# Reordering the first four tiles of a two-layer linear-attention kernel on all engines

## What is computed

```python
def layer(x, emb, mask, ...):            # twice; B=32 blocks of 128 rows, D=512, emb 32x1024
    xn = layernorm(x) * norm_scale + norm_bias
    q, k, v = xn @ Wq + bq, xn @ Wk + bk, xn @ Wv + bv
    k = masked(k); v = v * valid         # masked rows out
    q = softmax(q, within each head)     # 16 heads in layer 0, 8 in layer 1
    k = softmax(k, over the 128 rows)
    y = q @ (k^T @ v)                    # per head
    scale, shift = split(silu(emb) @ W_film + b_film)
    h = silu(layernorm(y) * film_scale... * (1 + scale) + shift)
    return x + h @ W_out + b_out
```

## Time and profile before

| | before |
|---|---|
| median of 3 runs | 858.17 us (856.25 to 859.12) |
| the profiled execution: its time | 857.14 us |
| its span, first to last instruction | 855.1 us |
| TensorE busy | 838.2 us (98%), 6659 matmuls |
| VectorE, ScalarE, GpSimd busy | 679.3, 603.1, 548.9 us |
| granted TensorE clock, mean | 1.00 |
| DMA, mean over the span | 199 GB/s |

### The profile page before, as it was taken

How to read it: one execution, slowest core, us unless ns; L and a number is a source line. 1 busy time by engine, 2 the same in 40 slices (tenths; PEclk the granted TensorE clock), 3 DMA queues, 4 the chain that set the end, 5 groups by cost and what they waited for, 6 DMA issues and landing times.

```text
span 855.1 us, 20095 instructions
## 1 busy us (share of the span) xinstructions
PE 838.2 (98%) x6659; PEld 719.9 (84%) x6659; DVE 679.3 (79%) x1362; ACT 603.1 (71%) x1442; POOL 548.9 (64%) x741
## 2 busy tenths in 40 slices
PE   7999999999999999999999999999999999999998
PEld 7778888888888888888878888888888888888886
DVE  6987778778788788778887887787788787787766
ACT  5376687686676776686876886776776686676665
POOL 3467766766766666766767667667667666765641
PEclk9999999999999999999999999999999999999999
DMA  8876676766667756555587556656566656566441
GB/s 309 286 225 201 201 218 199 228 216 205 195 210 208 233 197 199 179 165 175 169 247 233 185 172 200 201 180 201 179 204 201 202 186 189 178 194 211 142 160 62
DMA packets 139404, 169.81 MB, mean 199 GB/s; under 512 B 12302, under 2 KB 112006, under 8 KB 139302
## 3 DMA queue, kind: packets, MB, share of 16 engines
q1 hardware_dynamic: 138512, 167.56, 62.5%
q10 hardware_dynamic: 790, 0.98, 0.4%
HBM read 95.61 MB, written 72.88 MB: 197 GB/s over the span
## 4 chain that ended last, share of the span: by engine, by line
PE 83%; DMA 6%; DVE 4%; issue 2%; SPq 2%; POOL 1%; ACT 1%; DVEq 0%; POOLq 0%; ACTq 0%
PE PS L1152 72%; PE PS L1248 6%; PE PS L1232 3%; DMA X<-in_x 2%; DMA XT<-x_turned 1%; DMA x_turned<-XS 1%; DMA k_turned<-KT 1%; DMA QT<-qy_turned 1%; POOL XL L667 0%; SPq L400 0%; PE PS L1322 0%; DMA EK<-k_turned 0%; DVE BNX L1515 0%; PE PS L1276 0%; PE PS L1291 0%
## 5 line engine op out<-in xcount | busy, mean ns | idle before, releaser
L680 POOL TENSOR_TENSOR HL<-H,HH 128x512 fp32r<-128x512 f32 x60 | 77.5, 1292 | 185.3 <-ACT HH L916 185.3
L867 ACT ACTIVATE Z<-QT,FC,FA 128x128 f32<-128x128 f32 x240 | 99.0, 483 | 87.7 <-DMA QT<-qy_turned 87.7
L1152 PE MATMUL PS<-XH,WH_k 128*128 128x256 f32 x512 | 149.8, 293 | 0.7 <-DVE KN L1581 0.7
L1152 PE MATMUL PS<-XL,WH_k 128*128 128x256 f32 x512 | 144.8, 283 | 0.0
L1152 PE MATMUL PS<-XH,WL_k 128*128 128x256 f32 x512 | 144.8, 283 | 0.0
L953 ACT ACTIVATE XN<-X,NBX,RSX 128x512 f32<-128x512 f32 x60 | 48.8, 813 | 85.5 <-POOL NBX L629 85.5
L829 ACT ACTIVATE SK<-SK,KN 128x128 f32<-128x128 f32 x256 | 98.9, 387 | 10.7 <-DVE KN L1581 10.4
L1152 PE MATMUL PS<-WH_o,HH 128*128 128x512 f32 x248 | 101.3, 408 | 2.0 <-issue 1.9
L1152 PE MATMUL PS<-WH_v,XH 128*128 128x512 f32 x256 | 100.8, 394 | 0.0
L1152 PE MATMUL PS<-WH_q,XH 128*128 128x512 f32 x256 | 100.7, 393 | 0.0
L1152 PE MATMUL PS<-WL_v,XH 128*128 128x512 f32 x256 | 100.3, 392 | 0.0
(11 more groups left out here) (171 smaller groups left out, 2106.6 us busy)
## 6 DMA issues: line engine op xcount, KB each, us to landing
qy_turned<-QS SPq DMA_DIRECT2D x60, 512.0 KB, 2.9
QT<-qy_turned SPq DMA_DIRECT2D x240, 128.0 KB, 3.1
EK<-k_turned SPq DMA_DIRECT2D x128, 128.0 KB, 2.8
x_turned<-XS SPq DMA_DIRECT2D x30, 512.0 KB, 3.3
XT<-x_turned SPq DMA_DIRECT2D x120, 128.0 KB, 3.5
k_turned<-KT SPq DMA_DIRECT2D x52, 256.0 KB, 3.8
out_x<-X SPq DMA_DIRECT2D x31, 256.0 KB, 3.2
X<-in_x SPq DMA_DIRECT2D x11, 512.0 KB, 5.3
```

Source lines behind the costliest of these rows:

```text
L680: eng.tensor_tensor(hl_of(o), h_of(o), hh_of(o).bitcast(F32), ALU.subtract).then_inc(pool_hl, 1)
L867: z = eng.activation(z_of(o)[:, c * P:c * P + P].rearrange("p (q n) -> p q n", q=Q), src, ACT.Identity, bias=FC[l][:, c, b:b + 1], scale=F ...
L1152: mm = eng.matmul(dst, left[a](c), right[b](c), start=(c == 0 and a + b == 0), stop=(c == C - 1 and a == 1))
```

## The change

The order of the first four tiles is rewritten on SP, POOL, ACT, PE and DVE. The lists after step 4 stay. Two things are new besides order: chunks 2 and 3 of the key weights are cast by VectorE (`split_high` in its block, semaphore `dve_w`), and five low halves, (0, 0), (0, 1), (1, 0), (1, 1) and (2, 1) of (matrix, chunk), go from VectorE to GpSimd. Mask 1 is loaded by SP instead of ACT. ACT's own loads keep their queue, in another order. The fillers on PE are 10, 1 and 14 instead of 10, 14 and 2.

```diff
--- before.py
+++ after.py
@@ -172,7 +172,7 @@
         pe_tq, pe_ty, pe_a = sem("pe_tq"), sem("pe_ty"), sem("pe_a")
         pe_att, pe_y, pe_film = sem("pe_att"), sem("pe_y"), sem("pe_film")
         pe_fold, act_cp = sem("pe_fold"), sem("act_cp")
-        act_cond, act_w = sem("act_cond"), sem("act_w")
+        act_cond, act_w, dve_w = sem("act_cond"), sem("act_w"), sem("dve_w")
         act_ek, act_eq, act_z, act_t = sem("act_ek"), sem("act_eq"), sem("act_z"), sem("act_t")
         act_v, act_hh, act_xf, act_xh = sem("act_v"), sem("act_hh"), sem("act_xf"), sem("act_xh")
         dve_v, dve_q, pool_xl = sem("dve_v"), sem("dve_q"), sem("pool_xl")
@@ -338,11 +338,20 @@
             elif c == 0:
                 eng.wait_ge(ld_w[w - 1], 16)
 
+        def wait_high(eng, w, c):
+
+            if w == 0 and c >= C // 2:
+                eng.wait_ge(dve_w, c - C // 2 + 1)
+            elif w == 0:
+                eng.wait_ge(act_w, c + 1)
+            else:
+                eng.wait_ge(act_w, C * w - C // 2 + c + 1)
+
         def split_low(eng, w, chunks):
 
             for c in chunks:
                 wait_weights(eng, w, c)
-                eng.wait_ge(act_w, C * w + c + 1)
+                wait_high(eng, w, c)
                 eng.tensor_tensor(WL[w % 4][:, c, :], STAGES[w][:, c, :], WH[w % 4][:, c, :].bitcast(F32),
                                   ALU.subtract).then_inc(low_w[w][c], 1)
 
@@ -502,26 +511,26 @@
             load_first(eng, [1])
             load_x(2)
             load_w(1)
-            load_bias(2)
+            load_w(2)
             load_bias(0)
             load_bias(1)
-            load_w(2)
             load_film(0)
+            load_mask(eng, 1)
             load_x(3)
             wait_split(1)
-
             load_x(4)
+            wait_split(0)
+            load_w(3)
+            load_bias(2)
             write_qy(1)
-            load_film(1)
             write_keys(0)
             read_qy(1)
             place_keys(0)
-            wait_split(0)
-            load_w(3)
+            load_film(1)
+            write_qy(2)
             write_x(2)
-            write_qy(2)
+            read_qy(2)
             read_x(2)
-            read_qy(2)
             write_qy(3)
             write_x(3)
             masks_at(2)
@@ -691,28 +700,33 @@
 
             root_x(0)
             root_x(1)
+            split_low(eng, 0, [0])
+            split_low(eng, 0, [1])
             mask_of_keys(0)
+            split_low(eng, 1, [0])
             root_x(2)
             root_x(3)
+            split_low(eng, 1, [1])
             split_low(eng, 2, [0])
+            split_low(eng, 2, [1])
             normalise_keys(0)
+            mask_of_keys(1)
             queries(0)
+            normalise_keys(1)
             root_x(4)
-            mask_of_keys(1)
-            normalise_keys(1)
             root_x(5)
+            queries(1)
             root_x(6)
-            queries(1)
             normalise_keys(2)
             root_x(7)
+            queries(2)
+            add_bo(0)
             root_x(8)
-            add_bo(0)
-            queries(2)
             root_x(9)
             add_bo(1)
+            split_low(eng, 3, [1])
+            x_low(4)
             root_y(0)
-            x_low(4)
-            split_low(eng, 3, [1])
             normalise_keys(3)
             x_low(5)
             root_y(1)
@@ -960,24 +974,21 @@
                     eng.activation(CTH[n], COND[:, n * D:n * D + D], ACT.Tanh, scale=0.5).then_inc(act_cond, 1)
 
             eng.dma_start(VR, vec_rows).then_inc(ld_vec, 16)
+            load_first(eng, [2])
             load_first(eng, [3])
-            load_first(eng, [2])
             load_mask(eng, 0)
-            eng.dma_start(COND, cond).then_inc(ld_cond, 16)
             eng.dma_start(MI, mask0).then_inc(ld_mask, 16)
             eng.dma_start(MF, mask1).then_inc(ld_mask, 16)
+            eng.dma_start(COND, cond).then_inc(ld_cond, 16)
             split_high(0, [0])
             split_high(0, [1])
-            split_high(0, [2])
-            split_high(0, [3])
             x_turned(0)
             x_turned(1)
             split_high(1, [0])
             split_high(1, [1])
-            cond_tanh()
             split_high(1, [2])
             split_high(1, [3])
-            load_mask(eng, 1)
+            cond_tanh()
             split_high(2, [0])
             split_high(2, [1])
             split_high(2, [2])
@@ -987,22 +998,22 @@
             x_turned(3)
             exp_k(1)
             norm_x(4)
-            exp_k(2)
             norm_x(5)
             conditioning_sums(0)
-            exp_q(0)
+            exp_k(2)
             values(0)
+            values(1)
             norm_x(6)
             norm_x(7)
-            heads(0)
-            values(1)
+            exp_q(0)
             split_high(3, [0])
             split_high(3, [1])
+            exp_k(3)
             split_high(3, [2])
+            heads(0)
             values(2)
-            exp_k(3)
+            x_turned(4)
             norm_y(0)
-            x_turned(4)
             norm_x(8)
             heads(1)
             exp_q(1)
@@ -1365,30 +1376,23 @@
                 mm.then_inc(pe_valid, 1)
 
             eng.wait_ge(pool_const, 2)
-            keep_busy(B_Q, 4)
-            keep_busy(B_Q, 6)
+            keep_busy(B_Q, 10)
+            turn_vectors()
+            keep_busy(B_Q, 1)
             turn_x(0)
-            turn_vectors()
             turn_x(1)
-            keep_busy(B_Q, 2)
-            keep_busy(B_Q, 2)
-            keep_busy(B_Q, 2)
-            keep_busy(B_Q, 2)
-            keep_busy(B_Q, 2)
-            keep_busy(B_Q, 2)
-            keep_busy(B_Q, 2)
+            keep_busy(B_Q, 14)
             keys(0)
             keys(1)
-            keep_busy(B_Q, 2)
+            turn_valid()
+            values(0)
             turn_x(2)
-            turn_valid()
+            turn_x(3)
+            count()
             queries(0)
-            values(0)
+            values(1)
             queries(1)
-            turn_x(3)
-            values(1)
             turn_cond()
-            count()
             keys(2)
             conditioning(0)
             queries(2)
@@ -1729,6 +1733,12 @@
                     last = eng.tensor_scalar(FC[l][:, here, :], G[:, here, :], 0.5, None, ALU.mult)
                 last.then_inc(dve_film, 1)
 
+            def split_high(w, chunks):
+
+                for c in chunks:
+                    wait_weights(eng, w, c)
+                    eng.tensor_copy(WH[w][:, c, :], STAGES[w][:, c, :]).then_inc(dve_w, 1)
+
             def start():
 
                 eng.wait_ge(pool_const, 4)
@@ -1777,62 +1787,59 @@
                 eng.wait_ge(pe_vec, 1)
                 eng.tensor_copy(VC[:, :], PS[:, B_TY, 0:2 * VROWS]).then_inc(dve_vec, 1)
 
+            start()
             stat_x(0)
             stat_x(1)
             norm_x(0)
-            split_low(eng, 0, [0])
+            start_vectors()
             norm_x(1)
-            split_low(eng, 0, [1])
+            split_high(0, [2])
+            split_high(0, [3])
             split_low(eng, 0, [2])
-            start_vectors()
+            x_low(0)
             split_low(eng, 0, [3])
+            x_low(1)
             stat_x(2)
             stat_x(3)
-            x_low(0)
-            x_low(1)
-            split_low(eng, 1, [0])
+            split_low(eng, 1, [2])
+            norm_x(2)
+            split_low(eng, 1, [3])
             start_masks()
-            norm_x(2)
             norm_x(3)
-            split_low(eng, 1, [2])
             keys(0)
-            split_low(eng, 2, [1])
+            start_valid()
             split_low(eng, 2, [2])
-            split_low(eng, 1, [3])
             split_low(eng, 2, [3])
-            split_low(eng, 1, [1])
+            values(0)
             keys(1)
             key_sums(0)
-            queries(0)
-            stat_x(4)
-            values(0)
-            turn_queries(0)
-            stat_x(5)
-            stat_x(6)
-            start()
-            start_cond()
             x_low(2)
             x_low(3)
-            start_valid()
+            queries(0)
             turn_keys(0)
             key_sums(1)
+            start_cond()
+            turn_queries(0)
+            turn_keys(1)
+            values(1)
             start_cond_turned()
+            stat_x(4)
             queries(1)
-            turn_keys(1)
+            stat_x(5)
             zero_attention()
             keys(2)
-            values(1)
             start_count()
             turn_queries(1)
             turn_x(4)
+            turn_x(5)
             key_sums(2)
-            turn_x(5)
+            stat_x(6)
+            queries(2)
             stat_x(7)
+            keys(3)
+            values(2)
             stat_x(8)
             stat_x(9)
-            queries(2)
-            values(2)
-            keys(3)
             mixed(0)
             turn_queries(2)
             conditioning(0)
```

## The result

The changed kernel takes 868.35 us (median of 4 runs, 865.84 to 869.63) against 858.02 (4 runs, 856.25 to 859.12) before: a ratio of 1.0112, 95% interval 1.0092 to 1.0133. It is slower, and by more than the forecast's upper end of 863.6. The profiled execution took 865.84 us, its span is 864.1, TensorE is busy for 839.7 us of it.

A forecast was written before the change was run, and what follows sets the result against it. TensorE, 98% busy, was taken as the bound, so the start of keys(4) shifts everything: 67.6 instead of 64.97, with handovers plus 2.7 us, giving 859.8 profiled and 860.9 median. Range 857.0 to 863.6.

The forecast's parts named there:

- The sign: Whole kernel: the change makes it slower, by plus 2.7 us.
- The film load costs the write of x its lead: SyncE's queue: 2 MB ahead of write_x(2); turned x arrives at 56.0, 1.9 us earlier than before, not 3.8.
- serial line: Turned x to keys(4): x_turned(4), x_low(4), root_y(0), norm_y(0) now run one after another; keys(4) at 67.6 instead of 64.97.
- the part on mix(0): Start of mix(0): heads(0) done at 51.0, mix(0) 0.9 us earlier, TensorE waiting 3.7 us for 0.77.
- minus 5.6, with idle time the same within 0.7, so 46.5: VectorE before mix(0): less work ahead of keys(3) makes it end at 46.5 instead of 52.36.
- 0.9 in keys(0): VectorE: allowance of 0.9 us, in keys(0) alone, for time lost beside GpSimd's low halves.
- five low halves fewer (... 3.25): VectorE before keys(3): five low halves moved to GpSimd save VectorE 3.25 us.
- rival 3: Start of mix(0): heads(0) done by 48, turned x back by 50, lead stays, about 854.4; chance 0.07.
- VectorE has no idle time between 18 and 47: VectorE: the argument against the faster rival, no idle time to win keys(3) 3 us sooner from.
- Neither moves keys(4): VectorE slowed beside GpSimd's low halves, 0.85 or up to 1.3 us each: keys(4) said not to move.
- I find no wait on this way: TensorE up to attention(0): 33.6 us from 13.7 without a wait, attention(0) done at 47.3, 3.8 us ahead.
- Rival 2: keys(4) and neighbours, 62.9 to 67.6: TensorE's clock falls after idle times, 2 to 3 us more, 863.5; chance 0.12.

The follow-up runs named there:

- film_early: Changed kernel with load_film(1) issued by SyncE right behind load_bias(2) instead of behind place_keys(0); ratio 1.0082 against before.
- before_film: Kernel before with load_film(1) issued behind place_keys(0), ahead of the output weights and the write of turned x; ratio 1.0061 against before.
- before_y: Kernel before with x_turned(4) ahead of norm_y(0) on ScalarE and x_low(4) ahead of root_y(0) on GpSimd; ratio 1.0086 against before.
- second trace: Kernels before and after each run once more unchanged, one run each; keys(4) at 65.11 in before and 69.85 in after.
- low_back: Changed kernel with the five low halves back on VectorE, the rest of the change kept; ratio 1.0096 against before.
- heads_early: Changed kernel with heads(0) on ScalarE right behind exp_q(0), ahead of the output chunks and exp_k(3); ratio 1.0124 against before.
- y_first: Changed kernel with norm_y(0) ahead of x_turned(4) on ScalarE and root_y(0) ahead of x_low(4) on GpSimd; ratio 1.0064 against before.
- y_first_fillers: y_first with twenty fillers between attention(0) and mix(0); ratio 1.0025 against before.
- before_wo: Kernel before with the output weights loaded right behind x4 instead of behind place_keys(0); ratio 0.9987 against before.
- best: all_three with root_y(0) also ahead of add_bo(1) on GpSimd and six fillers before mix(0); ratio 1.0022 against before.
- all_three: Changed kernel with the edits of film_early, y_first and heads_early together; ratio 1.0047 against before.

## Why the prediction was wrong

**What held.** The sign, and the mechanism. keys(0) came at 12.4 with its second pair of chunks at 13.7 (forecast 13 and 13.7), keys(1) ended near 19 (19.5). The film load costs the write of x its lead (film_early and before_film; 1.7 to 4.2 us at turned x, by the traces compared). The orders of x and y make a serial line of 11.9 us for 11.6, and undone they give back 3.65 at keys(4); before_y shows 3.95 for them alone. keys(4) waits for x_low(5), and output(0) shifts with film(0).

**The step that failed** is VectorE's sum in the part on mix(0): "minus 5.6, with idle time the same within 0.7, so 46.5". It was 49.56, 3.1 us later. (The terms give 46.7; 0.2 of it is arithmetic.) The idle time was about right. After x_low(1), up to the end of keys(3), VectorE waits 2.06 us in before and 2.38 in after. What the sum lacked is that instructions grow long beside GpSimd's. It had this once, as 0.9 in keys(0), which before has too. Three more places cost 3.0 us in after: norm_x(3) 1.51 for 0.55 beside the low half (1, 1); start_cond's two 1.08 and 1.52 for 0.67 each beside queries(0) and normalise_keys(1); the last of keys(3) 0.96 for 0.16 beside queries(2). The second trace has the same (1.50, 1.08 and 1.52, 0.96). The first two, 2.2 us, lie ahead of turn_queries(0), which ends at 34.13 for 31.8, and of stat_x(7), 2.4 late. That GpSimd is the cause is shown for norm_x(3), and for KB, which low_back brings back to 0.53 and 0.16; for the others it is argued from what ran beside them. VectorE's timeline of before, for comparison:

```profile
33.41 0.67 DVE L1756 SCALAR_TENSOR_TENSOR XS<-Z,XS 32x512 f32<-32x512 f32 x1
34.01 0.67 DVE L1756 SCALAR_TENSOR_TENSOR XS<-EQ,XS 32x512 f32<-32x512 f32 x1
...
49.96 0.69 DVE L1620 TENSOR_TENSOR VV<-PS,BB 128x512 f32<-128x512 f32 x1 [0.80 <-PE PS L1152]
```

Nor did the term "five low halves fewer (... 3.25)" buy anything in the new order: low_back has them back and ends at the same time, because without them VectorE waits for other engines. And rival 3's "VectorE has no idle time between 18 and 47" is not what before shows: its waits there come to 1.1 us.

From there it went three ways:

- *To the queue.* turn_queries(0) was late, so write_qy(1) went out at 34.16 for 31.8, and behind it load_film(1) at 41.35 for 38.6. write_qy(2) and write_x(2) wait for transposes of their own on the same late VectorE: turn_x(5) ends at 43.80 and write_x(2) goes out at 43.83, for 41.2. The film half landed at 51.6 for 48.4 and the write of x, which was forecast 2.0 behind it, at 53.6 for 50.4. Then read_x(2), behind read_qy(2), at 54.23 for 51.2. Turned x came 3.6 late, and with the 0.3 on the serial line keys(4) was 3.8 late. In the second trace of after the issues are later still (41.67 and 44.26) but the film half lands 9.1 us after its issue and the write of x 8.6, so turned x is 1.65 late and keys(4) 2.25. The lateness of the issues is there in both; how long the transfer behind them takes is not settled by one trace. "Neither moves keys(4)" was said of VectorE's lateness with only heads(0) in view; I had not followed it through turn_queries(0) and turn_x(5) into SyncE's list. No run here has these transposes on time, so what their lateness costs at keys(4) is read from the traces and not tested.
- *To mix(0).* stat_x(7) over at 46.9 for 44.5, norm_x(7) at 48.45 for 45.8, heads(0) 2.4 late, TensorE's wait 4.53 for 3.7. This costs nothing by itself in after (heads_early). Nor does it matter that attention(0) was done at 48.9 for 47.3: "I find no wait on this way" missed three waits of 1.3 us in sum, the longest 0.82 for start_cond.
- *To the clock.* Rival 2's event happened, but not at its place: it wanted the low clock between mix(1) and keys(4), and it came after mix(0), from 52 to 59, hidden by the wait for x. The Trainium skill (TensorE: Matmul & The Clock Gate, Part 1) says that idleness brings the clock down; the 0.50 after 4.53 us without a matmul agrees.

**The account.** The forecast for the profiled execution was 859.8 and it took 865.84: 3.8 of the 6.0 us are at keys(4), 1.0 in the longer wait of output(0), counted as a shift but not as a new wait, and 1.2 in the tiles behind. The median lies 2.5 us above this execution, not 1.03 as in before: 1.5 more. The second trace took 867.03, 7.2 more than forecast, and divides otherwise: 2.25 at keys(4), 1.4 at output(0), 3.6 in the tiles behind. So the failed step accounts for at most half of the 7.5 us between the forecast median and the measured one, and a part of 2.7 (1.2 and 1.5) to 3.6 us has no cause that I can name.

**What the orders cost in sum.** Of 6.5 us at keys(4) in the first trace of after, 3.65 go with the y orders (y_first), a further 0.96 with the low clock (y_first_fillers). The last 1.86 are turned x: x_turned(4) starts at 59.82 in y_first_fillers for 57.97 in before, and mix(1) follows it by 3.5 us in both. TensorE's own work, behind the late heads(0), would have let mix(1) start only 0.39 earlier, so an earlier x alone would not have brought it all back.

**What stays open.** Whether the rest behind keys(4) (790.1 to 794.7 us) depends on the order of the start or only scatters: after shows 792.7 and 794.7, before 790.1 and 791.0, before_wo 792.5, and best, at full clock, 794.3. The six fillers of best were not tried alone.

## What to carry to other kernels

A late instruction has to be followed into every list that waits for it: here VectorE's transposes, some 2.4 us late, held the DMAs of SyncE's list, while the wait that was looked at cost nothing. Where a transfer and an engine's work meet in a hand-written order, the work that is ready first goes first (root and norm of y in the shadow of x's transfer were worth 3.7 us at keys(4) in one direction, 4.0 in the other). Moving work off an engine pays only if that engine has no wait behind it: ask first what it would wait for next. Where two engines slow each other, count it at every place where they now meet, and not only at the work that was moved.

## What was not expected of the hardware

- GpSimd beside VectorE stretches more than operations with two inputs in SBUF: norm_x(3), one tensor in and one out, took 1.51 us beside a low half (0.55 else). The Trainium skill (SBUF — State Buffer, Who interferes with whom) names such two-port modes, and a lock held for a whole instruction; the 1.51 agrees with that, and so does the 0.53 of low_back, where no low half runs beside it. GpSimd pays too: its normalise_keys(1) took 1.49 us beside start_cond; normalise_keys(3) took 1.04.
- TensorE's clock fell to 0.50 after a wait of only 1.46 us (all_three, behind attention(0), whose products have 32 columns), and stayed at 1.00 after 1.43 in heads_early and with six fillers in such a wait (best): what makes the difference between the first two is open. In the second trace of before it was 0.56 from 8 to 10 us and 0.66 from 35 to 40, with keys(4) at 65.11, 0.14 later than in the first.
